# One bank pair for the scores, part of the maxima inside the steps, and x1 measured a body later

## The reference

```python
x = x + tanh(g_xattn) * mha(layernorm(x), ctx, ctx)      # 16 heads of 32
h = layernorm(x)
xq = fake_quant(h, clip_x)                               # scale: sigmoid(clip) * max|h| / 127, over all of h
h2 = fake_quant(silu(xq @ Wg.T) * (xq @ Wu.T), clip_down)
x = x + tanh(g_ffn) * (h2 @ Wd.T)                        # Wg, Wu, Wd rounded row by row in the same way
```

## Time and profile before

| | kernel before |
|---|---|
| runs | 1901.03 us (1897.21 to 1904.65) |
| profiled execution | 1898.31 us, of it span 1896.1 |
| TensorE busy | 1645.5 us, 87% |
| VectorE busy | 1402.2 us, 74% |
| ScalarE, GpSimd busy | 813.1 us, 516.7 us |
| granted clock of TensorE, mean | 0.951 |
| attention bodies 2 to 15 | 191.8 to 1269.7 us of the span |

### The profile page before, as it was taken

One profiled execution on the slowest core, in us unless ns is written; L12 is line 12 of the kernel. 1 busy time (PEld: TensorE's weight loads), 2 busy tenths in 40 slices (PEclk: granted clock), 3 DMA queues, 4 the chain that ended last, 5 costly groups with the idle time before them and its releaser, 6 DMA issues.

```text
span 1896.1 us, 34665 instructions
## 1 busy us (share of the span) xinstructions
PE 1645.5 (87%) x11820; PEld 782.3 (41%) x11868; DVE 1402.2 (74%) x1853; ACT 813.1 (43%) x1068; POOL 516.7 (27%) x782
## 2 busy tenths in 40 slices
PE   3769989989999899998999899986599999989787
PEld 2224434434344344443444434433344444434333
DVE  6627687787877868768778687786778778878565
ACT  2223524325144152342432514324677777756242
POOL 6212414324133242331422423112000000006644
PEclk7979999999999999999999999998799999999899
DMA  6445454454444444445445444315235453115997
GB/s 190 127 119 116 121 147 110 121 138 120 126 109 121 135 119 125 115 119 148 110 121 127 128 126 93 94 55 204 89 142 192 166 214 140 45 45 212 340 420 301
DMA packets 271525, 274.48 MB, mean 145 GB/s; under 512 B 156720, under 2 KB 205872, under 8 KB 268848
## 3 DMA queue, kind: packets, MB, share of 16 engines
q1 hardware_dynamic: 271408, 272.73, 47.4%
HBM read 126.10 MB, written 62.39 MB: 99 GB/s over the span
## 4 chain that ended last, share of the span: by engine, by line
issue 63%; POOL 13%; DVE 9%; PE 6%; DMA 4%; SPq 2%; POOLq 1%; ACT 0%; DVEq 0%; ACTq 0%
DMA x<-out_dram 4%; DVE rs L873 3%; POOL ol L545 3%; POOL xres L552 3%; POOL yh L600 3%; PE bank L1264 2%; DVE mx L881 2%; SPq L358 1%; PE bank L1165 1%; POOL nw L527 1%; PE bank L1167 1%; PE bank L1166 1%; POOLq L259 1%; POOL nw L525 1%; POOL nw L529 1%
## 5 line engine op out<-in xcount | busy, mean ns | idle before, releaser
L873 DVE RECIPROCAL rs<-bank 128x256 f32<-128x256 f32 x128 | 224.5, 1754 | 125.7 <-POOL ol L545 105.5
L639 ACT ACTIVATE pr<-spair 128x1024 f32<-128x1024 f32 x256 | 258.9, 1019 | 112.0 <-PE spair L1246 112.0
L881 DVE TENSOR_REDUCE mx<-spair 128x4 f32<-128x1024 f32 x256 | 300.0, 1213 | 0.0
L632 ACT ACTIVATE parts<-bank,bqk 128x512 f16<-128x512 f32 x128 | 87.9, 687 | 293.9 <-PE bank L1167 293.9
L1264 PE MATMUL bank<-pr,v 128*32 128x256 f32 x2048 | 140.5, 392 | 54.8 <-DVE o L875 54.8
L1361 PE MATMUL spair<-xqT,wgT 128*128 128x512 bf16 x684 | 179.5, 382 | 2.8 <-ACT xqT L747 1.8
L1361 PE MATMUL spair<-xqT,wuT 128*128 128x512 bf16 x691 | 179.9, 381 | 0.7
L860 DVE SCALAR_TENSOR_TENSOR parts<-bank,bqk,parts 128x512 f16<-128x512 f32 x128 | 95.1, 748 | 114.6 <-ACT parts L632 114.6
L1246 PE MATMUL spair<-stacks 128*128 128x256 f16 x1024 | 154.1, 277 | 7.8 <-DMA stacks<-mT 7.3
L1165 PE MATMUL bank<-xT,wqT 128*128 128x512 f16 x256 | 103.2, 403 | 58.8 <-issue 24.7
L730 ACT ACTIVATE sil<-spair,gsc 128x512 f32<-128x512 f32 x176 | 118.1, 680 | 75.2 <-PE spair L1361 75.2
(11 more groups left out here) (160 smaller groups left out, 3198.6 us busy)
## 6 DMA issues: line engine op xcount, KB each, us to landing
stacks<-parts SPq DMA_DIRECT2D x768, 64.0 KB, 2.0
x<-out_dram SPq DMA_DIRECT2D x32, 1024.0 KB, 11.2
h_spill<-hb SPq DMA_DIRECT2D x10, 2816.0 KB, 9.2
hb<-h_spill SPq DMA_DIRECT2D x10, 2816.0 KB, 15.2
xbuf<-in_x_dram SPq DMA_DIRECT2D x16, 1024.0 KB, 5.4
cbuf<-in_ctx_dram SPq DMA_DIRECT2D x16, 1024.0 KB, 6.0
xres<-in_x_dram SPq DMA_DIRECT2D x16, 1024.0 KB, 5.3
out_dram<-xres SPq DMA_DIRECT2D x16, 1024.0 KB, 4.3
```

What stands on the lines that cost most here:

```text
L639: act.activation(pr[:, u % 4, :, :, :].rearrange("p a b q -> p (a b q)"), spair[u % 2][:, :, :].rearrange("p a q -> p (a q)"), ACT.Exp, sc ...
L873: dve.reciprocal(rs[:, g % 2, :], obank[:, S:2 * S]).then_inc(recip_done, 1)
L881: dve.tensor_reduce(mx[:, h:h + 2, b, :], spair[u % 2][:, :, :].rearrange("p a (q k) -> p a q k", q=KH), AX_X, ALU.max).then_inc(max_done, 1)
```

## The change

Scores use only the first bank pair, so each waits for the exp before it. The first four units of maxima (heads 0 to 3 of both sequences) become `max_unit`s in the second bank pair alone; TensorE issues them in steps 1, 3, 4 and 5, and VectorE reads them in steps 2, 4, 5 and 6. Pairs 2 to 7 stay in the tail. In the tail two value products come ahead of pv 7, and the turning of the maxima ahead of the last output product. x1 goes to a buffer `x1b`; its statistics, roots, shifts and maxima are taken one body later, and the spread of it (scale, shift, absolute value, in place) is ScalarE's. Value copies go to ScalarE, without the bias, which now goes through the output weights into `tgbo` once at the start. `o32` has four buffers. The diff, cut to its core:

```diff
-                wait(sp, x1_stored, j * 16, alone=True)
-                wait(sp, x1_dev, j * NT, alone=True)
+
+                wait(sp, x1_ready, j * NT, alone=True)
                 sp.dma_start(xres[:, :, :], xg[j]).then_inc(res_in, 16)
 
             def store_x1(j):
                 wait(sp, x1_ready, j * NT + NT, alone=True)
-                sp.dma_start(og[j], xres[:, :, :]).then_inc(x1_stored, 16)
+                sp.dma_start(og[j], x1b[:, :, :]).then_inc(x1_stored, 16)
...
+            def body(j, before, nxt):
+                for g in range(NGR - 1):
+                    if nxt is not None and g < NT:
+                        low_c(nxt, g)
+                    if nxt is not None and g > NT:
+                        low_x(nxt, g - NT - 1)
                     if g > 0:
                         o_low(j, g - 1)
                     if g == 2 and nxt is not None:
                         x_rstds(nxt)
+                    if g == 4:
+                        residual(j, 0)
+                        residual(j, 1)
+                    if g == 5 and before is not None:
+                        x1_rstds(before)
+                    if g == 6:
...
+            def spread(j, t):
+
+                wait(act, x1_shift, 2 * j + 2)
+                wait(act, x1_stored, j * 16 + 16)
+                at = bass.ds(j * NT + t, 1)
+                act.activation(x1b[:, t, :], x1b[:, t, :], ACT.Abs, scale=rstd2[:, at],
+                               bias=shift2[:, at]).then_inc(x1_spread, 1)
...
                 exps(j, 0)
                 exps(j, 1)
-                if i is not None:
-                    qk_high(i, 1)
                 for g in range(NGR - 1):
                     exps(j, 2 * g + 2)
-                    exps(j, 2 * g + 3)
-                    if i is not None and g + 2 < 8:
-                        qk_high(i, g + 2)
+                    if i is not None:
+                        qk_high(i, g + 1)
                     if g > 0:
                         o_high(j, g - 1)
+                    exps(j, 2 * g + 3)
...
+                if i is not None:
+                    v_copy(i, 0)
+                    v_copy(i, 1)
+                if before is not None:
+                    spread(before, 0)
+                    spread(before, 1)
                 o_high(j, NGR - 1)
                 if i is not None:
+                    v_copy(i, 2)
+                if before is not None:
+                    spread(before, 2)
+                    spread(before, 3)
+                if i is not None:
+                    v_copy(i, 3)
                     mT_copy(i)
...
-                if g >= 2:
-                    wait(dve, o_hi, j * NGR + g - 1)
-                    wait(dve, o_lo, j * NGR + g - 1)
+                if g >= 4:
+                    wait(dve, o_hi, j * NGR + g - 3)
+                    wait(dve, o_lo, j * NGR + g - 3)
...
+                dve.tensor_reduce(mx[:, h:h + 2, b, :], spair[1 if u < 4 else u % 2][:, :, :].rearrange("p a (q k) -> p a q k", q=KH),
...
+                wait(dve, x1_stored, j * 16)
+                wait(dve, x1_max, j * NT)
+                dve.scalar_tensor_tensor(out=x1b[:, t, :], in0=pj[(t) % 3][:, :],
                                          scalar=small[:, TGX256:TGX256 + 1], in1=xres[:, t, :],
...
+            def x1_top(j, t):
+                wait(dve, x1_spread, j * NT + t + 1)
+                dve.tensor_reduce(amax2[:, bass.ds(j * NT + t, 1)], x1b[:, t, :], AX_X, ALU.max).then_inc(x1_max, 1)
...
+            def body(i, j, before, nxt):
                 if i is not None:
                     qk_low(i, 0)
-                    qk_low(i, 1)
                 for g in range(NGR - 1):
+                    if i is not None and g == NGR - 2:
+                        qk_low(i, g + 1)
                     norm(j, g)
-                    if i is not None and g + 2 < 8:
-                        qk_low(i, g + 2)
+                    if i is not None and g < NGR - 2:
+                        qk_low(i, g + 1)
                     if nxt is not None:
...
+                    if i is not None:
+                        if g == 2:
+                            key_max(i, 0)
+                        if g == 4:
+                            key_max(i, 1)
+                        if g == 5:
+                            key_max(i, 2)
+                        if g == 6:
+                            key_max(i, 3)
+                    if nxt is not None:
+                        if g == 3:
+                            x_norm_tile(nxt, 0)
+                            x_norm_tile(nxt, 1)
+                        if g >= 5:
                             x_norm_tile(nxt, g - 3)
+                    if before is not None:
+                        if g == 2:
+                            x1_tile_stats(before, 0)
+                            x1_tile_stats(before, 1)
+                        if g == 3:
+                            x1_tile_stats(before, 2)
+                        if g == 4:
+                            x1_tile_stats(before, 3)
+                            x1_measure(before)
+                        if g == 6:
+                            x1_shifts(before)
...
                 if i is not None:
-                    key_max(i, 0)
-                    key_max(i, 1)
+                    key_max(i, 4)
+                    key_max(i, 5)
+                    if before is not None:
+                        x1_top(before, 0)
+                    key_max(i, 6)
+                    key_max(i, 7)
+                    if before is not None:
+                        x1_top(before, 1)
                 norm(j, NGR - 1)
-                if i is None:
+                if i is not None:
+                    key_max(i, 8)
+                    key_max(i, 9)
+                    if before is not None:
+                        x1_top(before, 2)
+                    key_max(i, 10)
+                    key_max(i, 11)
+                    if before is not None:
+                        x1_top(before, 3)
+                else:
                     weight_scale(0, IC)
                     weight_scale(1, 2 * IC)
-                for t in range(NT):
-                    if i is not None:
-                        v_copy(i, t)
-                        key_max(i, 2 + 2 * t)
-                        key_max(i, 3 + 2 * t)
+                    for t in range(NT):
+                        x1_top(before, t)
                 for t in range(NT):
                     if t == 2 and i is None:
                         weight_int(0)
-                    if t == 3:
-                        x1_tile_stats(j, 0)
-                        x1_tile_stats(j, 1)
                     x1_tile(j, t)
-                    if i is not None and t < 3:
-                        key_max(i, 10 + 2 * t)
-                        key_max(i, 11 + 2 * t)
-                x1_tile_stats(j, 2)
-                x1_tile_stats(j, 3)
...
-                    wait(pe, x1_ready, before * NT + (4, 2, 3)[g])
-                else:
-                    wait(pe, v_ready, (i - 1) * NT + (2, 3, 4)[g])
-                three(pj[g % 3][:, :],
...
                 if t < 3:
-                    wait(pe, qk_lo, i * 8 + 6 + t)
+                    wait(pe, qk_lo, i * 8 + (8, 6, 7)[t])
...
+            def max_unit(i, u):
+
+                b, half = u // 2, u % 2
+                if u == 0:
+                    wait(pe, qk_hi, i * 8 + 2)
+                wait(pe, max_done, i * NU + u)
+                for qh in range(KH):
+                    for a in range(2):
+                        rows = slice(DK * (2 * half + a), DK * (2 * half + a) + DK)
+                        last = pe.matmul(spair[1][:, a, qh * S:qh * S + S],
+                                         parts[rows, 0, 0, b * S + qh * P:b * S + qh * P + P],
+                                         parts[rows, 0, 2, b * S:b * S + S], start=True, stop=True)
+                last.then_inc(max_mm, 1)
...
-                if u >= 2:
-                    wait(pe, exp_done, j * NU + u - 1)
+                if u >= 1:
+                    wait(pe, exp_done, j * NU + u)
                 else:
-                    wait(pe, max_done, j * NU + 15 + u)
+                    wait(pe, max_done, j * NU + 15)
                 for a in range(2):
                     h = HPC * c + 2 * half + a
                     for kh in range(KH):
-                        last = pe.matmul(spair[u % 2][:, a, kh * S:kh * S + S],
+                        last = pe.matmul(spair[0][:, a, kh * S:kh * S + S],
...
                 if i is not None:
                     qk(i, 0, par, before)
                 score(j, 0)
-                score(j, 1)
                 if i is not None:
                     qk(i, 1, par, before)
+                score(j, 1)
                 for g in range(NGR - 1):
                     score(j, 2 * g + 2)
                     pv(j, g)
                     score(j, 2 * g + 3)
-                    if i is not None and g + 2 < 8:
```

(37 more changed lines are left out.)

220 lines of the change are left out of this document (124 added, 96 removed).

## The result

| | before | after |
|---|---|---|
| time, median of the runs | 1899.12 us (1894.54 to 1904.65, 4 runs) | 2028.3 us (2024.99 to 2029.57, 4 runs) |
| span of the profiled execution | 1896.1 us | 2027.6 us |
| mean granted clock | 0.951 | 0.931 |

The changed kernel is slower: ratio 1.066, 95% interval 1.063 to 1.069. The forecast was 2067 with a range from 1985 to 2110, so direction and mechanism held, and the size was 39 us too large.

What follows compares the result with a forecast made beforehand. TensorE, busy 87% of the span, was taken as the bound. Bodies 2 to 15 gave +157 us (stops, clock, back edges included), the first body +11, the rest 0: +168 in total, hence 2067 us, range 1985 to 2110.

Steps and rivals of the forecast that it cites:

- The stops: TensorE at units 2 and 3 waits for VectorE's previous maximum, 3.8 us each, 7.6 us a body.
- The clock behind them: Behind each stop, a spell at 1.2 GHz as at the back edge: 2.6 us each, 5.2 a body.
- half the spell: Variant of the rival that the clock stays up: 2028 us; stops with small or no spell had chance 0.14.
- The body without stops: One attention loop body: work 67.4 us plus waits of 1.1 and 4.2 us, 72.8 us.
- the tail: End of a body, from the end of pv 6: 29.5 us, 25.3 of TensorE's work and 4.2 of waits.
- The body with stops: One attention loop body: 72.8 us plus 7.6 of stops and 5.2 of clock, 85.6 us.
- The back edge: At the loop's branch, every second body: 3.5 us of branch plus 2.6 of low clock, 6.1 us, six times.
- the faster rival: Units 2 and 3 find their bank pair free, no stops: 1877 us, down to 1862; chance 0.06.
- First body, prologue and end: Outside bodies 2 to 15: +11 us for the first body, 0 for the rest with bounds -10 and +10.
- x transposed at 71 us: SyncE's last transpose of x some 71 us into a body: hidden over 80 us, level with one of 72.8.

Runs made afterwards that it cites:

- e1: The changed kernel with VectorE reading maxima 1, 2 and 3 ahead of the quotient of steps 4, 5 and 6; 1920.9 us.
- e2: The changed kernel with the following projection done once more on TensorE ahead of units 2 and 3, its result overwritten; 1967.9 us.
- e8: e1 with the fourth stack put behind the transposes and load of x and the row of maxima in SyncE's queue; 1850.4 us.
- e10: The changed kernel with its last pair of maxima between the third and fourth output product and the turning behind the fourth; 2064.1 us.
- e6: The kernel before with four output buffers for the quotients and nothing else of the change; 1876.4 us.
- e4: The changed kernel with the turning of the maxima behind the last output product instead of ahead of it; 2033.9 us.
- e13: e6 with the load of x issued behind the row of maxima, the store of x1 and the load of the residual; 1879.7 us.
- e3: The changed kernel with every unit of maxima behind the projection of its step instead of ahead of it; 1916.0 us.

## Why the prediction was right, and where its sizes were off

The forecast was +168 us, the profiled executions differ by 131.5. By its own steps:

- **The stops** were forecast at units 2 and 3, 3.8 us each, by a chain of 4.27 us from the end of pv. They are there and nowhere else, 3.59 each: 7.2 a body instead of 7.6. e1 shows that they are the cause.
- **The clock behind them** was taken from the back edge, 2.6 a stop. e2 gives 2.0, 4.1 a body instead of 5.2. The spell differs from stop to stop: in the body shown the step with the first took 10.93 us, the one with the second 12.23, where a step with a unit and no stop takes 5.86. That the measured 2028 is also the prediction's number for half the spell is chance: the spell was 2.0 of 2.6, and 33 of the 39 us are the back edge (below).
- **The body without stops** was 72.8 by the sum; e8 has 72.5. In the changed kernel the tail came to 29.0 from pv's end (855.77 to 884.76) against 29.5, but by other parts: 2.6 us of waits and not 4.2, and 26.4 of TensorE's own work and not 25.3. The value copies, taken at 0.7, took 0.58, and the units 0.33 and not 0.25.
- **The body with stops**, no back edge: 84.9 in the mean of eight, against 85.6. That is 10 us over 14 bodies.
- **The back edge** is the step that failed. I took 3.5 + 2.6 us for it, with the reason that with the last output product ahead of it no wait runs beside the branch. It is the reverse: with that product queued and every wait ahead of the branch met, the sequencer goes on to the branch, and the fetch lies under the product. The six bodies with a back edge take 85.5 in the mean, 0.6 more than the others: 33 us of the error. The prediction named this ("if the branch is fetched while the last product runs") but only beside the faster rival. The forecast's own picture is e10, where the wait is late: 2064, and 5.8 us a back edge. In the kernel before it was 3.4; in the bodies without a back edge a wait for x1 of up to 1.5 us stood at that place there.
- **First body, prologue and end.** +11 was forecast for the first body and 0, with bounds of 10, for what lies around. Up to the second copy +9.8 is found, but not as told. The first body starts when xT lands, 4.7 us later (113.23 against 108.57), as SyncE reaches the transposes of c 4.1 us later (90.47, 86.36). From there to the second copy it is 5.2 more (88.44, 83.26), although both stops of 3.59 us are in it. Behind the last copy it is 7.3 more, 4.1 of them ahead of the first gate product, where the longest wait of TensorE is 12.2 us for ScalarE's weight copies; before it was 7.7, for VectorE. No run took either apart; the causes stay open.
- **The rivals.** The faster one, 1877 down to 1862, decided at under 1.5 us of stop a body, happened in e8, at 1850, but only with SyncE's order changed. The prediction had x transposed at 71 us, level with such a body. It counted from the second stack's score; the queue has to be counted from the first stack (16.3 us in) and is 59.6 long, so it is 76. Thus e1 stayed at 1921.

A sentence on the branch: the Trainium skill, *Runtime: NRT & Kernel Launch*, Instruction fetch mechanics, has a taken branch wait for the fetch of instructions that are no longer held, and the traces agree, with 3.4 to 3.8 us in the median in every kernel here but e6. The 108 ns of *Advanced Engine Details and Errata* (the Trainium skill), Control Flow Timing, are in none of them at this loop. What the fetch costs the time, though, is 0.6 (after) to 5.8 us (e10) a back edge, by what the array still has to do.

## What to carry to other kernels

When work goes into a steady loop on a shared buffer, write both engines' lists for one step side by side: if the reader of the buffer stands behind something that waits for this step's own matmul, the writer stops for the whole chain, and moving the read ahead of it (e1) takes the stop away. Then count the DMA queue from its first issue to its last against the shorter body: what the next body needs first must not stand last in it (e8). At a loop's back edge leave the engine a long piece of work whose waits, and all waits ahead of the branch, are met early.

## What the runs showed of the hardware that was not expected

- TensorE's sequencer takes the branch while up to a whole product (2.6 us) is still to run: a branch of 3.4 to 3.9 us then leaves 1.0 to 1.7 us of idle, and the twelve matmuls behind it take 2.60 us at eleven of the twelve back edges of after and e4 (3.06 at the twelfth). Behind a wait met 0.32 us late it leaves 3.6 to 4.1 us, and the twelve take 3.9 to 5.1 (before, e10).
- The branch takes longer beside DMA traffic, as a fetch by DMA would: 5.13 to 6.13 us with a 1 MB load issued 1.2 to 1.6 us ahead of it (e6), 3.35 to 3.70 with that load moved away (e13).
- Behind stops of the same length, 3.59 us, it took 4.25 to 5.63 us from the unit to the next score, where 2.92 is the rule at full clock: 1.3 to 2.7 more. So it was for 27 of the 28 stops in bodies 2 to 15 of the changed kernel. Behind the 28th it took 2.92, and the clock kept 1.00, so a gap of that length doesn't fix the clock by itself. Waits of 1.00 us at the same places left the clock at 1.00 (e2, e3).

```profile
1264.73 0.39 PE L1311 MATMUL spair<-parts 32*128 32x256 f16 x4 [3.59 <-DVE mx L925]
...
1267.65 0.60 PE L1352 MATMUL spair<-stacks 128*128 128x256 f16 x4
```
```profile
1264.70:1267.70 3.00, 2.97 (x17) 1.35 (x18) 1.24 (x7) 0.00 (x0) 0.41 (x1) 1.00 0.82 90
```

- One matmul's length isn't enough to read the clock by. At a back edge of e13 the first matmul behind 3.84 us of idle (800.63) took 0.39 us, as at full clock, but eight of the next took 0.58 to 0.63, and the twelve 4.29 us.
